# Answers of the last layer's mixture of experts: scattered by token as they come, or stored by slot and gathered at the end

## The reference, cut to what matters

```
# mixture of the first half, for every token x
h   = silu(x @ W1[e]) * (x @ W3[e])            # 128 -> 256, e one of two experts
out = sum over the two e of  gate[e] * (h @ W2[e])       # 256 -> 128

# FFN, for every token t
h   = t @ mlp1_w[e] + mlp1_b[e]                # 128 -> 512: glu and lin, 256 each
h   = min(glu, 7) * sigmoid(1.702 * min(glu, 7)) * (clip(lin, -7, 7) + 1)
out = sum over the two e of  gate[e] * (h @ mlp2_w[e] + mlp2_b[e])
```

## Time and profile before

| | before |
|---|---|
| three executions, us | 943.21, 941.74, 945.5 |
| profiled execution, us | 934.72 |
| its span, first to last instruction, us | 933.4 |
| granted TensorE clock, mean | 0.862 |
| PE busy, us (share) | 692.4 (74%) |
| DVE busy, us | 592.3 (63%) |
| ACT busy, us | 398.4 (43%) |
| POOL busy, us | 283.3 (30%) |

### The profile page before, as it was taken

One profiled execution on the slowest core, in us unless ns is written; L12 is line 12 of the kernel. 1 busy time (PEld: TensorE's weight loads), 2 busy tenths in 40 slices (PEclk: granted clock), 3 DMA queues, 4 the chain that ended last, 5 costly groups with the idle time before them and its releaser, 6 DMA issues. The chain is left out here.

```text
span 933.4 us, 14335 instructions
## 1 busy us (share of the span) xinstructions
PE 692.4 (74%) x4255; PEld 515.2 (55%) x4255; DVE 592.3 (63%) x1590; ACT 398.4 (43%) x951; POOL 283.3 (30%) x294
## 2 busy tenths in 40 slices
PE   4999687725887489069959889999885988812991
PEld 2998646615666267058847655656453544501651
DVE  4797487457798211666686568889466777401675
ACT  3201344525643122444534457777652444501660
POOL 2372163520000554001000013545202650375552
PEclk9999888756899589579987999999975999955996
DMA  9980012211000410363037402222101331211215
GB/s 281 271 322 1 1 35 55 62 52 45 1 1 0 35 22 22 92 261 163 1 66 156 132 15 76 76 74 73 36 12 41 98 92 45 71 56 34 70 55 141
DMA packets 80730, 73.36 MB, mean 79 GB/s; under 512 B 9903, under 2 KB 75064, under 8 KB 80144
## 3 DMA queue, kind: packets, MB, share of 16 engines
q1 hardware_dynamic: 67232, 57.00, 21.1%
q0 software_dynamic: 6848, 12.38, 5.3%
q10 hardware_dynamic: 6576, 3.08, 1.2%
HBM read 42.83 MB, written 27.42 MB: 75 GB/s over the span
## 5 line engine op out<-in xcount | busy, mean ns | idle before, releaser
L3359 PE MATMUL banks<-weights,work 128*128 x156 | 90.5, 665 | 9.6 <-issue 8.3
L2535 DVE TENSOR_REDUCE work<-banks 128x2 f32<-128x512 f32 x128 | 82.9, 681 | 13.1 <-PE banks L2526 11.4
L3382 PE MATMUL banks<-weights,work 128*128 x312 | 54.1, 300 | 18.5 <-issue 12.1
L3372 PEld LDWEIGHTS banks<-consts,work 128*128 128x128 f32 x156 | 21.1, 151 | 83.0 <-issue 55.8
L3372 PE MATMUL banks<-consts,work 128*128 128x128 f32 x156 | 34.0, 302 | 35.2 <-issue 13.4
L3382 PEld LDWEIGHTS banks<-weights,work 128*128 128x128 f32 x312 | 44.9, 207 | 22.3 <-issue 21.5
L816 POOL DMA_INDIRECT xs<-t,idx x48 | 50.1, 1043 | 23.0 <-issue 11.9
L2526 PE MATMUL banks<-work 96*128 96x256 bf16 x256 | 48.6, 274 | 9.0 <-DVE work L2535 6.2
L3483 DVE TENSOR_SCALAR work<-banks,gate_of 128x128 f32<-128x128 f32 x39 | 13.6, 350 | 65.4 <-issue 39.6
L1196 POOL DMA_INDIRECT g<-rows,back_to x16 | 15.4, 961 | 120.7 <-DVE back_to L1922 116.1
L3527 POOL DMA_INDIRECT ys<-work,back_to x39 | 39.5, 1014 | 32.6 <-issue 15.5
(11 more groups left out here) (508 smaller groups left out, 1964.8 us busy)
## 6 DMA issues: line engine op xcount, KB each, us to landing
weights<-in_w SPq DMA_DIRECT2D x1, 6668.0 KB, 19.5
weights<-in_w SPq DMA_DIRECT2D x1, 4569.5 KB, 23.5
weights<-in_r SPq DMA_DIRECT2D x1, 2950.5 KB, 26.2
xs<-zero SPq DMA_DIRECT2D x1, 2600.0 KB, 25.0
xs<-zero SPq DMA_DIRECT2D x1, 2560.0 KB, 23.4
work<-xs SPq DMA_DIRECT2D x39, 65.0 KB
work<-xs SPq DMA_DIRECT2D x39, 64.0 KB
weights<-in_w SPq DMA_DIRECT2D x1, 2124.5 KB, 12.3
```

The costliest lines, as they stand in the source:

```text
L2535: v.tensor_reduce(self.mxb[:, 2 * h:2 * h + 2], self.n.bank(bank).rearrange("p (r n) -> p r n", r=2), AX, ALU.max, negate=True).then_inc(* ...
L3359: pe.matmul(self.mid(t), self.hT[t % 4], w1[:, bass.ds(off * 4, 512)], start=True, stop=True).then_inc(*self.prod1.up())
L3372: ins = pe.transpose(self.mid(m)[:, 128 * f:128 * f + 128], self.ha[m % 4][:, 128 * f:128 * f + 128], self.c["ident"])
L3382: ins = pe.matmul(self.y_bank(m), self.at_[m % 4][:, 128 * f:128 * f + 128], w2[:, bass.ds(self.pe_off[m] * 2 + 128 * f, 128)], start=(f = ...
```

## The change

Mixture answers are stored by their slots, plainly, 39 direct stores by SP into `ys[2]` (now 39 tiles long), unscaled. Row numbers and gates no longer travel with the rows; the four small POOL copies, ACT's two copies per tile and POOL's 39 scatters go. At the end POOL waits for all stores and gathers from `ys[2]` by 32 indirect gathers, two per token tile, in groups of 4, 4, 4, 1, 1, 1 and 1 token tiles; DVE does four instructions of 128 columns per token tile (times the first gate; plus the second answer times its gate; times `g`; plus `x`), and SP stores the output in seven pieces. `Back` goes.

The 32 gathers of the FFN's answers each wait until the one two ahead of them has landed, and DVE's pieces wait for the two gathers of their own token tile in place of those of four token tiles.

The FFN's second bias is added by PE: POOL splits it early into three bf16 parts in three partitions (eight instructions of 3 x 1024, after the last of its preparations at L2741), and a matmul of three ones rows by these parts opens each FFN tile's second product. PE waits once, at tile 0, for the parts. The FFN answer is moved to SBUF by ACT, scaled, between its `turned` and `silu` of the step, in place of DVE.

`FfnGate` begins 40 steps in, not 32.

```diff
...
+    def answer_bias(self):
+
+        n, g, G = self.n, self.gpsimd, self.G
+        rest, parts, ident = n.r3["mlp2_b"][0:3, :], n.answer_bias, self.c["ident"]
+        taken = (self.c["digit_sum"][0:3, 0:1], ident[0:3, 2:3])
+        g.tensor_scalar(rest, rest, LastExperts.ALPHA, None, ALU.mult).then_inc(*G.up())
+        for mask in taken:
+            g.wait_ge(*G.now())
+            g.tensor_copy(parts, rest).then_inc(*G.up())
+            g.wait_ge(*G.now())
+            g.tensor_scalar(parts, parts, mask, None, ALU.mult).then_inc(*G.up())
+            g.wait_ge(*G.now())
+            g.tensor_tensor(rest, rest, parts, ALU.subtract).then_inc(*G.up())
+        g.wait_ge(*G.now())
+        g.tensor_copy(parts, rest).then_inc(*n.answer_bias_made.up())
...
+    def pair_stored(self, t):
+
+        g = t // 2
+        return self.stored[g % 7].at(2 * (g // 7) + 1)
...
+    def store(self, eng, t):
         n = self.n
-        if t % 2 == 0 and t >= 14:
-            eng.wait_ge(*self.ffn_stored(t - 14))
+        if t >= 14 and (t % 2 == 0 or t == self.FFN):
+            eng.wait_ge(*self.pair_stored(t - 14))
         eng.wait_ge(*self.y.at(t))
-        eng.dma_start(n.ys[3][t * P:(t + 1) * P, :], self.yb[t % self.RETURNS]).then_inc(*self.stored[t // 2 % 7].up())
+        ys, r = (n.ys[3], t) if self.ffn(t) else (n.ys[2], t - self.FFN)
+        eng.dma_start(ys[r * P:(r + 1) * P, :], self.yb[t % self.RETURNS]).then_inc(*self.stored[t // 2 % 7].up())
 
     def ffn_fetched(self, t):
-        return self.fetched[t // 4].at(7)
...
-        for t in range(self.TILES):
+        for t in range(self.TILES + 7):
             rows(t + 8)
-            if 0 <= t - 7 < self.BY_SYNC:
-                self.ffn_store(sp, t - 7)
+            if 0 <= t - 7 < self.BY_SYNC or t - 7 >= self.FFN:
+                self.store(sp, t - 7)
...
+        if m == 0:
+            pe.wait_ge(*self.n.answer_bias_made.at(0))
+        if self.ffn(m):
+            pe.matmul(self.y_bank(m), self.n.bf16_ones[0:3, :].bitcast(BF16)[:, 0:128], self.n.answer_bias[:, bass.ds(self.pe_off[m], 128)],
+                      start=True, stop=False)
         for f in range(2):
             ins = pe.matmul(self.y_bank(m), self.at_[m % 4][:, 128 * f:128 * f + 128], w2[:, bass.ds(self.pe_off[m] * 2 + 128 * f, 128)],
-                            start=(f == 0), stop=(f == 1))
+                            start=(f == 0 and not self.ffn(m)), stop=(f == 1))
...
-        if not self.ffn(t):
-            k = t - self.FFN
-            a.activation(self.n.back_to[:, k:k + 1], self.rows[t % 8][:, C:C + 1], ACT.Copy).then_inc(*self.to.up())
-            a.activation(self.n.gate_of[:, k:k + 1], self.rows[t % 8][:, C + 1:C + 2], ACT.Copy).then_inc(*self.to.up())
...
+    def act_y(self, m):
+        a = self.scalar
+        self.free_answer(a, m)
+        a.wait_ge(*self.prod2.at(m))
+        a.activation(self.yb[m % self.RETURNS], self.y_bank(m), ACT.Copy, scale=1.0 / self.ALPHA).then_inc(*self.y.up())
...
+            if self.ffn(t - 4):
+                self.act_y(t - 4)
...
         v.wait_ge(*self.prod2.at(m))
-        if self.ffn(m):
-            v.scalar_tensor_tensor(out=self.yb[m % self.RETURNS], in0=self.y_bank(m), scalar=1.0 / self.ALPHA,
-                                   in1=n.r3["mlp2_b"][:, bass.ds(self.dve_off[m], 128)], op0=ALU.mult, op1=ALU.add).then_inc(*self.y.up())
-        else:
-            k = m - self.FFN
-            v.wait_ge(*self.told(m))
-            v.tensor_scalar(self.yb[m % self.RETURNS], self.y_bank(m), n.gate_of[:, k:k + 1], None, ALU.mult).then_inc(*self.y.up())
+        v.tensor_copy(self.yb[m % self.RETURNS], self.y_bank(m)).then_inc(*self.y.up())
...
-        for t in range(NT):
-            for j in range(2):
-                g.indirect_dma_start(self.ffn_rows[j][:, t, :], None, n.ys[3][:, :], bass.IndirectOffsetOnAxis(
-                    ap=n.routes[1][0][:, j, t:t + 1], axis=0)).then_inc(*self.fetched[t // 4].up())
-        for t in range(self.FFN, self.TILES):
-            k = t - self.FFN
-            if k % 2 == 0 and k >= 14:
-                g.wait_ge(*self.returned(t - 14))
-            g.wait_ge(*self.told(t))
-            g.wait_ge(*self.y.at(t))
-            g.indirect_dma_start(n.ys[2][:, :], bass.IndirectOffsetOnAxis(ap=n.back_to[:, k:k + 1], axis=0), self.yb[t % self.RETURNS], None,
-                                 bounds_check=n.ys[2].shape[0] - 1, oob_is_err=False).then_inc(*self.row_out[k // 2 % 7].up())
+        for k in range(2 * NT):
+            t, j = divmod(k, 2)
+            if k >= 2:
+                g.wait_ge(*self.fetched[(k - 2) % 4].at((k - 2) // 4))
+            g.indirect_dma_start(self.ffn_rows[j][:, t, :], None, n.ys[3][:, :], bass.IndirectOffsetOnAxis(
+                ap=n.routes[1][0][:, j, t:t + 1], axis=0)).then_inc(*self.fetched[k % 4].up())
...
+    GROUPS = ((0, 1, 2, 3), (4, 5, 6, 7), (8, 9, 10, 11), (12,), (13,), (14,), (15,))
...
+    def pool(self):
+        n, g = self.n, self.gpsimd
+        for s in self.sources:
+            g.wait_ge(*s)
+        for u, group in enumerate(self.GROUPS):
+            for t in group:
+                for j in range(2):
+                    g.indirect_dma_start(self.rows[j][:, t, :], None, n.ys[2][:, :], bass.IndirectOffsetOnAxis(
+                        ap=n.routes[0][0][:, j, t:t + 1], axis=0)).then_inc(*self.fetched[u].up())
+        yield
+
     def dve(self):
-        n, v, D = self.n, self.vector, self.D
-        v.wait_ge(*D.now())
-        for q in range(4):
-            four = slice(4 * q, 4 * q + 4)
-            t, x = n.t1[:, four, :], n.x[:, four, :]
-            v.wait_ge(*self.got.done(4 * q))
-            v.tensor_tensor(t, self.rows[0][:, four, :], self.rows[1][:, four, :], ALU.add).then_inc(*D.up())
-            v.wait_ge(*D.now())
-            v.tensor_tensor(t, t, n.g[:, four, :], ALU.mult).then_inc(*D.up())
-            v.wait_ge(*D.now())
-            v.tensor_tensor(x, x, t, ALU.add).then_inc(*self.made.up())
+        n, v, D, gates = self.n, self.vector, self.D, self.n.routes[0][1]
+        v.wait_ge(*D.now())
+        for u, group in enumerate(self.GROUPS):
+            v.wait_ge(*self.fetched[u].at(2 * len(group) - 1))
+            for t in group:
+                a, b, x = self.rows[0][:, t, :], self.rows[1][:, t, :], n.x[:, t, :]
+                v.tensor_scalar(a, a, gates[:, 0, t:t + 1], None, ALU.mult).then_inc(*D.up())
+                v.wait_ge(*D.now())
+                v.scalar_tensor_tensor(out=a, in0=b, scalar=gates[:, 1, t:t + 1], in1=a, op0=ALU.mult, op1=ALU.add).then_inc(*D.up())
+                v.wait_ge(*D.now())
+                v.tensor_tensor(a, a, n.g[:, t, :], ALU.mult).then_inc(*D.up())
+                v.wait_ge(*D.now())
+                v.tensor_tensor(x, x, a, ALU.add).then_inc(*self.made.up())
             yield
 
     def sp(self):
         n, sp = self.n, self.sync
-        for q in range(4):
-            sp.wait_ge(*self.made.at(q))
-            sp.dma_start(n.out[:, 4 * q:4 * q + 4, :], n.x[:, 4 * q:4 * q + 4, :]).then_inc(*self.stored.up())
-            yield
-        sp.wait_ge(*self.stored.at(3))
+        for u, group in enumerate(self.GROUPS):
+            sp.wait_ge(*self.made.at(group[-1]))
+            part = slice(group[0], group[-1] + 1)
+            sp.dma_start(n.out[:, part, :], n.x[:, part, :]).then_inc(*self.stored.up())
...
-    gate = FfnGate(n, ffn_rows, experts.ffn_fetched, sent2.done(), 32, 2)
+    gate = FfnGate(n, ffn_rows, experts.ffn_fetched, sent2.done(), 40, 2)
     n.run(Opening(n, norm, n.turn, mix, experts), gate)
     rows = [n.work[:, i * 2048:(i + 1) * 2048].rearrange("p (t c) -> p t c", c=C) for i in range(2)]
-    got = Back(n, rows, n.ys[2], experts.done(), "mix", both=True)
-    n.run(got)
-    n.run(Ending(n, rows, got))
+    n.run(Ending(n, rows, experts.done()))
 
 
 def build(nc, ins, out):
```

More of the change, by code:

```diff
@@ L206, in __init__ @@
         tiles = (24, 1, 40, 40)
-        self.xs = [dt(f"xs{n}", (t * P, C + (1, 0, 2, 0)[n]), F32, kind="Internal").ap() for n, t in enumerate(tiles)]
-        self.ys = [dt(f"ys{n}", (t * P, C), F32, kind="Internal").ap() for n, t in enumerate((16, 32, 32, 39))]
+        self.xs = [dt(f"xs{n}", (t * P, C + (1, 0, 0, 0)[n]), F32, kind="Internal").ap() for n, t in enumerate(tiles)]
+        self.ys = [dt(f"ys{n}", (t * P, C), F32, kind="Internal").ap() for n, t in enumerate((16, 32, 39, 39))]
         self.rows = dt("rows", (TOK, C), F32, kind="Internal").ap()
@@ L3265, in xT_done @@
         return self.xT_d.at(t) if t < self.EARLY else self.xT.at(t - self.EARLY)
[L3267 to L3280 removed]
+    def pair_stored(self, t):
+        g = t // 2
+        return self.stored[g % 7].at(2 * (g // 7) + 1)
     def ffn_done(self):
[L3283 removed]
+        return [self.pair_stored(t) for t in range(26, self.FFN, 2)]
     def done(self):
[L3286 to L3288 removed]
+        return [self.pair_stored(t) for t in range(64, self.TILES, 2)]
+    def store(self, eng, t):
```

(26 more changed lines are left out.)

45 lines of the change are left out of this document (20 added, 25 removed).

## The result

The change makes the kernel slower: 947.56 us against 939.85 (medians of 20 runs each), ratio 1.0076 with the interval 1.0053 to 1.0099, 7 to 8 us more where 14 us less were forecast. Two runs of after that fell in a slower state, at 954.66 and 954.28 us, are left out of the ratio. The profiled executions are 946.45 and 934.72 us. Four marks divide them: the first `silu` of an FFN tile behind its table load, the first and the last mixture answer, and the end.

The account below looks back on a forecast made before the run. Bounds: last-layer expert tiles, a hole in them (PE completions told late while POOL issues unpaced gathers), and the end. Last answer 870.8 plus end 48.4 gives span 919.2, 920.5 with 1.3 around it; -14.2 on 943.21: 929 us, range 920 to 962.

Parts of the forecast that it names:

- They follow 434.6, and POOL is idle 68.96 us ahead of 503.50: free: Ahead of the last layer: POOL's eight bias-split instructions, 28 to 40 us, fit in POOL's idle time and cost nothing.
- rival D: At the end: gathers beside DVE's instructions are dearer, 32 x 0.30 = +10 us, giving 939 us; chance 0.08.
- The wait of two in flight: FFN gathers: POOL waits on landings, 1.4 us per gather against 1.26 before, 45 us in all, ending at 850.
- The residual of 3 us: Mixture tiles: what the paced FFN gathers still cost PE, between nothing and the whole hole, taken as 3 us.
- A: Mixture tiles: the pause in answers beside the FFN gathers is mostly gone, 929 us (920 to 942); chance 0.45.
- B: Mixture tiles: half the pause stays, PE at half pace, 22.5 us in place of 3, giving 948.5; chance 0.20.
- C: Mixture tiles: the whole pause stays despite POOL's wait, 960 to 967 us, 962 the likeliest; chance 0.25.
- The end: From the last mixture answer to the span's end: 48.4 us with the new gathers, 29.1 more than before.
- The FFN tiles: Last layer's FFN tiles: bias matmul and answers on ACT cost -7 to +10 us, taken as +2.
- C's eighth answer: Mixture tiles, if the pause stays: eighth answer at 848 to 855, 4.2 to 7.0 us behind the last gather.
- The gain of the hole: Mixture tiles: without the pause beside POOL's unpaced gathers, the last answer comes at 870.8 against 914.09, 43.3 us earlier.

Follow-up runs that it names:

- e1: Before with the eight POOL instructions of the bias split added, result unused: 943.54 against 936.16 us, ratio 1.0081.
- e2: After with only one cast left of the POOL bias split, so its answers carry a wrong bias: 931.16 us, ratio to before 0.9936.
- e3: After with no wait between its 32 FFN gathers, as before had them: ratio to before 1.0297.
- e10: The kernel of e5 again, on a chip like the first: 925.29 us against 933.97 for before, ratio 0.9900.
- e15: The kernel of e5 and e10 once more, in another series: 926.73 us against 935.6 for before, ratio 0.9894.
- e12: Before with no POOL work added, but 13 DVE instructions of 256 columns in layer 2: 944.35 against 935.6 us, ratio 1.0108.
- e8: Before, unchanged, run again for its trace on a chip like the first; no time of its own is given.
- e5: After without bias split and bias matmul, FFN answers moved by DVE, a rest after every fourth FFN gather; on another chip, 0.9930 to 0.9988 of before.
- e7: After with one FFN gather in flight in place of two, on the odd chip: ratio to before 1.0461.

## Why the prediction was wrong

*The step that failed* is "They follow 434.6, and POOL is idle 68.96 us ahead of 503.50: free". The length was overestimated (28 to 40 us; it took 16.5) and the cover was read from the wrong engine: I looked at whether POOL was free, not at what DVE does beside it. The price is 4.8 us of DVE held up, and with what follows 7.6 (e1) in the time. Without the split the change is at 0.9936 of before (e2); part of that is not the split's, since e2's mixture tiles are 4 to 9 us shorter than after's, for a reason that no run shows. The same text reckons in rival D with POOL and DVE slowing each other, and looks for it at the end only.

*The wait of two in flight* was right in kind, POOL waits for its own landings, 1.55 us a gather against 1.4. The residual of 3 us was mis-sized: the mixture takes 79.0 and 74.1 us in the two traces of after where 67.3 was forecast, 7 to 12 more. That is between A and B (B: 22.5 for the residual). C, the slower rival, is refuted for the change as it is and confirmed for unpaced gathers by e3. So no rival has what made it slower: B's mechanism, that part of the hole stays, gives 9 of the 22 us between forecast and result, and the largest other part, the split, stands in no rival. That the measured 947.56 lies inside the range and 1 us from B's 948.5 is luck.

*The end*: 48.4 us forecast, 52.1 and 50.8 measured. The sum holds in each term but the last: from the last gather to the end it took 10.0 and 8.2 us where 6.3 were set, since DVE's four instructions were costed at 1.4 us without the lateness that the first part of the same text describes for PE. D (gathers dearer beside DVE) is not what came: they took 1.27 us each.

*The FFN tiles*: +2 forecast, +3.4 by the means over the traces but the odd chip's.

*Two readings* were off and changed nothing: layer 1 has 20 gathers from 309.37 to 333.40, not 16, and C's eighth answer could come up to 857 (850 and 7.0), not 855.

Together, with the two traces of after averaged: split 8.7, FFN 1.4, mixture 9.2, end 3.0, 22.3 us over the forecast of -14.2, or +8.1; measured +7 to +8. The gain of the hole, which the forecast rested on, did come, 33.6 of the 45.3 us forecast in after itself; e10 and e15 turn it into a faster kernel, at 0.99 of before.

## What to carry to other kernels

An instruction put into an engine's idle time is free only if it holds up no engine beside it: look at what DVE does there before POOL is given elementwise work, and don't take a delay in a stretch on the path to cost its own length alone, since more was lost behind it in each trace here. A long row of indirect DMAs from POOL needs rests, or another engine's completions arrive late; a rest after every fourth was enough here. When a mechanism is found, run it through every stretch of the new kernel, the new end too.

## What the runs showed of the hardware

- POOL's subtraction of 3 x 1024 elements in fp32 (2.13 us) holds a DVE instruction with two SBUF inputs for its whole length: 2.27 us in place of 0.43; its cast of as many (1.11 us) did so too, 1.25 us. POOL's time here goes by columns, not partitions: three partitions of 1024 columns took 2.1 to 2.9 us (1.0 to 1.1 for a cast), 128 partitions of 256 columns 0.87.
- A delay of 5.9 us on DVE at 450 us cost 10.1 us in the time (5.9 to 14.3; e12), and the granted clock in 480 to 500 was 0.66 in place of 0.74.
- Beside an unbroken row of gathers 1.26 us apart, an idle DVE waited up to 22.7 us for a product that PE had ended (e8, which is before again; 18.6 in e3), an idle ACT up to 16.2 (before), and DVE up to 2.3 us for its own last instruction (after).
- One of the chips shows less of this at the same density: no such wait of DVE in the end of e5 and e7, and in layer 1 one of 4.4 us in place of 12.1. The kernel before took 899 us on it in place of 934 to 940.
- A gather of 64 KB with none other in flight took 2.97 us on average from one issue to the next (2.73 to 3.90, e7), two in flight 1.55 us each.
